# An attention kernel on one core: four key slots of one unit in four turned by DMA moves and VectorE instead of TensorE transposes

## What is computed

```python
# layer 0: x is (8, 512, 32, 32), 8 heads of 64 channels, n = 1024 pixels
hn = group_norm(x, gn1_scale, gn1_bias)
qkv = einsum('bchw,oc->bohw', hn, w_qkv) + b_qkv
q, k, v = split(qkv.reshape(b * 8, 3 * 64, n), 3, axis=1)
wgt = softmax(einsum('bct,bcs->bts', q * scale, k * scale), axis=-1)
a = einsum('bts,bcs->bct', wgt, v).reshape(b, c, h, w)
out = group_norm(einsum('bchw,oc->bohw', a, w_proj) + b_proj, gn2_scale, gn2_bias)
x = x + out
# layer 1: one head over 512 channels, weights normalised, RMS norm, residual
```

## Time and profile before

| | us |
|---|---|
| median of 3 runs | 3390.89 |
| lowest and highest | 3390.49, 3391.6 |
| the profiled execution | 3391.86 |
| its span, first to last instruction | 3389.7 |
| TensorE matmuls busy | 3361.0 |
| VectorE busy | 2125.2 |
| ScalarE busy | 1830.0 |
| GpSimd busy | 1063.3 |

### The profile page before, as it was taken

How to read it: one execution, slowest core, us unless ns; L and a number is a source line. 1 busy time by engine, 2 the same in 40 slices (tenths; PEclk the granted TensorE clock), 3 DMA queues, 4 the chain that set the end, 5 groups by cost and what they waited for, 6 DMA issues and landing times.

```text
span 3389.7 us, 51772 instructions
## 1 busy us (share of the span) xinstructions
PE 3361.0 (99%) x16752; PEld 2767.7 (82%) x16752; DVE 2125.2 (63%) x3468; ACT 1830.0 (54%) x3082; POOL 1063.3 (31%) x946
## 2 busy tenths in 40 slices
PE   7999999999999999999999999999999999999999
PEld 4888888888888888888888888888888888888887
DVE  4677456773578735786457864578555784557844
ACT  3677226772278623785237843388333883247822
POOL 0345113441044410354104531145211552124511
PEclk9999999999999999999999999999999999999999
DMA  8512245222544025341153322542224422343212
GB/s 322 164 38 63 94 124 138 67 59 78 134 120 95 32 93 150 88 100 74 45 157 99 82 75 64 155 100 63 78 76 141 100 63 94 86 140 74 63 56 75
DMA packets 109849, 332.10 MB, mean 98 GB/s; under 512 B 21744, under 2 KB 54768, under 8 KB 98800
## 3 DMA queue, kind: packets, MB, share of 16 engines
q1 hardware_dynamic: 107632, 322.15, 33.2%
q10 hardware_dynamic: 1920, 6.29, 0.9%
HBM read 162.68 MB, written 31.49 MB: 57 GB/s over the span
## 4 chain that ended last, share of the span: by engine, by line
PE 92%; DMA 2%; DVE 2%; ACT 1%; SPq 1%; issue 1%; POOL 0%; ACTq 0%; DVEq 0%; POOLq 0%
PE big L473 26%; PE big L606 14%; PE ops L592 14%; PE tps L577 14%; PE big L702 7%; PE big L613 5%; PE tps L773 4%; PE ops L773 4%; PE ops L556 3%; DMA ST<-ST 2%; PE big L516 1%; SPq L446 1%; DVE HL L1336 0%; DVE XA L1331 0%; SPq L389 0%
## 5 line engine op out<-in xcount | busy, mean ns | idle before, releaser
L1033 POOL TENSOR_SCALAR PB<-PB,small 128x1024 f32<-128x1024 f32 x576 | 648.1, 1125 | 1297.2 <-DVE small L1263 1279.4
L1257 DVE TENSOR_REDUCE small<-big 128x1 f32<-128x1024 f32 x512 | 625.0, 1221 | 85.1 <-PE big L606 82.0
L1268 DVE TENSOR_TENSOR PT<-tps,PT 128x512 fp32r<-128x512 f32 x1024 | 651.9, 678 | 42.0 <-ACT PT L894 41.7
L894 ACT ACTIVATE PT<-tps 128x512 fp32r<-128x512 f32 x1024 | 563.7, 596 | 159.2 <-PE tps L577 156.2
L888 ACT ACTIVATE PB<-big,small 128x1024 f32<-128x1024 f32 x512 | 572.2, 1118 | 93.6 <-DVE small L1257 90.6
L592 PE MATMUL ops<-PT,VT 128*128 128x512 f32 x2048 | 599.0, 414 | 0.0
L606 PE MATMUL big<-ST 128*128 128x512 f32 x2048 | 554.2, 392 | 2.7 <-DMA ST<-ST 2.7
L577 PEld LDWEIGHTS tps<-ident,PB 128*128 128x128 f32 x4096 | 470.3, 140 | 95.2 <-DVE PT L1268 31.3
L577 PE MATMUL tps<-ident,PB 128*128 128x128 f32 x4096 | 545.7, 274 | 0.9
L606 PEld LDWEIGHTS big<-ST 128*128 128x128 f32 x2048 | 382.6, 188 | 90.7 <-issue 5.5
L592 PEld LDWEIGHTS ops<-PT,VT 128*128 128x128 f32 x2048 | 346.1, 189 | 47.2 <-DVE PT L1268 5.0
(11 more groups left out here) (158 smaller groups left out, 4775.5 us busy)
## 6 DMA issues: line engine op xcount, KB each, us to landing
ST<-ST SPq DMA_DIRECT2D x360, 256.0 KB, 5.0
W<-d_qk SPq DMA_DIRECT2D x32, 1024.0 KB, 5.9
W<-PB SPq DMA_DIRECT2D x256, 128.0 KB, 2.4
XA<-in_x SPq DMA_DIRECT2D x8, 2048.0 KB, 7.6
X<-in_x SPq DMA_DIRECT2D x8, 2048.0 KB, 9.2
W<-d_wp SPq DMA_DIRECT2D x8, 2048.0 KB, 11.8
W<-d_g SPq DMA_DIRECT2D x8, 2048.0 KB, 12.2
W<-d_m SPq DMA_DIRECT2D x8, 2048.0 KB, 7.8
```

The source lines that it names most:

```text
L894: act_fn(pt_slot(u, s)[:, 0, :], tps[n % 2][:], ACT.Copy).then_inc(s_pt_hi, 1)
L1033: nc.gpsimd.tensor_scalar(PB[:, i, :], PB[:, i, :], rinv[:, i:i + 1], 1.0, ALU.mult, ALU.mult)\
L1257: V.tensor_reduce(negmax[:, i:i + 1], tile(("s", 4 * u + tb))[:], axis=AX.X, op=ALU.max, negate=True).then_inc(s_row_max, 1)
L1268: V.tensor_tensor(pt_slot(u, s)[:, 1, :], tps[n % 2][:], pt_slot(u, s)[:, 0, :].bitcast(f32), ALU.subtract).then_inc(s_pt_ready, 1)
```

## The change

Units 0, 4 and 8 of a batch (`MOVED`, the first unit of pairs 0 to 2) have their slots 4 to 7, the upper 512 keys, turned in another way. `move_quarters` lets SyncE issue, for each such unit, two parts of 16 transfers: part 0 when two blocks of probabilities are normalised, part 1 when all four are. One transfer copies 32 partitions by 2 blocks by 128 elements. They go from PB to F0, which is the lower half of X. When both parts are there, VectorE transposes in blocks of 32 (`square`) into the upper half of X: slots 4 and 5 in step 6 of the group of 16, slots 6 and 7 in step 8. `moved_hi` on ScalarE and `moved_lo` on VectorE then write the two parts in the same steps. TensorE skips the 16 transposes of these slots.

So that a row of 128 elements of a transfer holds what one partition quarter needs of all four slots, the upper 512 keys of pairs 0 to 2 are stored in another order (`keys_by_turn`): the four slots alternate with stride four. The other units of these pairs, which are still turned by TensorE, read their slots 4 to 7 with stride four.

X is now in use during pairs 0 to 2, so x is loaded behind slot 71 of the batch and behind `stack_head(b, 3, 0)`, and GpSimd scales it in steps 50, 52, 54 and 56.

```diff
+MOVED = [4 * pair for pair in range(PAIRS - 1)]
+MOVED_SLOTS = [8 * u + s for u in MOVED for s in range(4, NT)]
+def moved_pair(step):
+    n = 16 * (step // 16) + {6: 4, 8: 6}.get(step % 16, 0)
+    unit = 4 * (step // 16)
+    return (8 * unit + n % 16, 8 * unit + n % 16 + 1) if n % 16 and unit in MOVED else ()
-X_SCALE_STEPS = (20, 23, 26, 29)
+X_SCALE_STEPS = (50, 52, 54, 56)
+        F0 = X[:, 0:2, :].rearrange("p a (b n) -> p (a b) n", n=HALF).rearrange("p q (t n) -> p q t n", t=KB)
+        def squared(s):
+            return X[:, 2 + (s - 4) // 2, HALF * (s % 2):HALF * (s % 2) + HALF]
+        def keys_by_turn(pair, half, row):
+            if half and 4 * pair in MOVED:
+                return row.rearrange("p (q r s) -> p s q r", q=QUARTERS, s=4)
+            return row.rearrange("p (s q r) -> p s q r", q=QUARTERS, s=4)
+            def move_quarters(b, u):
+                for part in range(2):
+                    sp.wait_ge(s_p_norm, b * 72 + 4 * u + 2 * part + 2)
+                    own_wait(sp)
+                    if u and part == 0:
+                        sp.wait_ge(s_squared, squared_count(b, 8 * (u - 4) + NT - 1))
+                        own_wait(sp)
+                    rows = slice(2 * part, 2 * part + 2)
+                    for tq in range(QUARTERS):
+                        for sq in range(QUARTERS):
+                            sp.dma_start(F0[32 * sq:32 * sq + 32, tq, rows, :],
+                                         PB[32 * tq:32 * tq + 32, rows, HALF + P * sq:HALF + P * sq + P])\
+                              .then_inc(s_moved[part], 16)
-                sp.dma_start(X[:], src_x(b)).then_inc(s_x_res, 16)
+                move_quarters(b, 0)
                 sp.wait_ge(s_v_full, b * 4 + 4)
...
                 stack_head(b, 1, 1)
+                move_quarters(b, 4)
                 stack_head(b, 2, 0)
                 stack_head(b, 2, 1)
+                move_quarters(b, 8)
                 stack_head(b, 3, 0)
+                sp.wait_ge(s_pt_ready, b * 144 + MOVED_SLOTS[-1] + 1)
+                own_wait(sp)
+                sp.dma_start(X[:], src_x(b)).then_inc(s_x_res, 16)
...
-                                                   PB[:, 4 * (u % 2) + t, P * s:P * s + P], ident[:])
+                        row = PB[:, 4 * (u % 2) + t, :]
+                        if s >= 4 and u // 4 * 4 in MOVED:
+                            keys = row[:, HALF:N].rearrange("p (k s) -> p s k", s=4)[:, s - 4, :]
+                        else:
+                            keys = row[:, P * s:P * s + P]
+                        last = nc.tensor.transpose(tps[n % 2][:, P * t:P * t + P], keys, ident[:])
...
-                    if n >= 0:
+                    if n >= 0 and n not in MOVED_SLOTS:
                         transposes(n // 8, n % 8)
                         transposes(n // 8, n % 8 + 1)
...
                     if last_values(step):
                         last_v_hi(last_values(step))
+                    for n in moved_pair(step):
+                        moved_hi(n)
...
+                def square(n):
+                    u, s = n // 8, n % 8
+                    if s == 4:
+                        for part in range(2):
+                            dve.wait_ge(s_moved[part], (b * len(MOVED) + MOVED.index(u) + 1) * EXCHANGE)
+                    V.transpose(squared(s).rearrange("p (t q r) -> p t q r", t=KB, q=QUARTERS),
+                                F0.rearrange("p q t (r s) -> p s t q r", s=4)[:, s - 4, :, :, :])\
+                     .then_inc(s_squared, 1)
...
-                    if n >= 0:
+                    if n >= 0 and n not in MOVED_SLOTS:
                         pt_lo(n // 8, n % 8)
                         pt_lo(n // 8, n % 8 + 1)
+                    for n in moved_pair(step):
+                        square(n)
+                    for n in moved_pair(step):
+                        moved_lo(n)
```

More of the change, by code:

```diff
@@ L218, in build @@
         s_ld_u = sem("ld_u")
+        s_moved = [sem(f"moved{i}") for i in range(2)]
+        s_squared = sem("squared")
+        s_values_read = sem("values_read")
         s_stack_a = sem("stack_a")
@@ L574, in transposes @@
                     if n >= 2:
-                        pe.wait_ge(s_pt_ready, b * 144 + n - 1)
+                        bank_read = n - 2 if n - 2 not in MOVED_SLOTS else n - 6
+                        pe.wait_ge(s_pt_ready, b * 144 + bank_read + 1)
                     for t in range(4):
-                        last = nc.tensor.transpose(tps[n % 2][:, P * t:P * t + P],
-                                                   PB[:, 4 * (u % 2) + t, P * s:P * s + P], ident[:])
+                        row = PB[:, 4 * (u % 2) + t, :]
[4 more added lines that the diff above has]
+                        last = nc.tensor.transpose(tps[n % 2][:, P * t:P * t + P], keys, ident[:])
                     last.then_inc(s_t_full, 1)
@@ L593, in values0 @@
                                   start=(s == 0 and part == 0), stop=(s == 7 and part == 1))
+                    if n + 4 in MOVED_SLOTS:
+                        last.then_inc(s_values_read, 1)
                     if s == 7:
@@ L879, in qk_hi @@
                         act.wait_ge(s_stack_b, (b * PAIRS + pair) * 96)
-                    act_fn(unstacked(what, 0)[:, HALF * half:HALF * half + HALF], t[:, 0:HALF], ACT.Identity,
+                    to, of = unstacked(what, 0)[:, HALF * half:HALF * half + HALF], t[:, 0:HALF]
+                    if what:
+                        to, of = keys_by_turn(pair, half, to), of.rearrange("p (s q r) -> p s q r", q=QUARTERS, s=4)
+                    act_fn(to, of, ACT.Identity,
                            bias=(bq, bk)[what][:, pair:pair + 1])\
@@ L887, in exps @@
                     i = 4 * (u % 2) + tb
+                    if u - 2 in MOVED and tb == 0:
+                        for part in range(2):
+                            act.wait_ge(s_moved[part], (b * len(MOVED) + MOVED.index(u - 2) + 1) * EXCHANGE)
                     act_fn(PB[:, i, :], t[:], ACT.Exp, bias=negmax[:, i:i + 1], accum_out=rowsum[:, i:i + 1])\
@@ L1248, in qk_lo @@
                     cols = slice(HALF * half, HALF * half + HALF)
-                    V.scalar_tensor_tensor(unstacked(what, 1)[:, cols], tile(("qk", j))[:, 0:HALF],
-                                           (bq, bk)[what][:, pair:pair + 1],
-                                           unstacked(what, 0)[:, cols].bitcast(f32), ALU.add, ALU.subtract)\
-                     .then_inc(s_nat_ready, 1)
+                    to, of, hi = unstacked(what, 1)[:, cols], tile(("qk", j))[:, 0:HALF], unstacked(what, 0)[:, cols]
+                    if what:
+                        to, hi = keys_by_turn(pair, half, to), keys_by_turn(pair, half, hi)
+                        of = of.rearrange("p (s q r) -> p s q r", q=QUARTERS, s=4)
+                    V.scalar_tensor_tensor(to, of, (bq, bk)[what][:, pair:pair + 1], hi.bitcast(f32),
+                                           ALU.add, ALU.subtract).then_inc(s_nat_ready, 1)
                 def row_max(u, tb):
@@ L1269, in pt_lo, with moved_lo @@
                                     ALU.subtract).then_inc(s_pt_ready, 1)
+                def square(n):
+                    u, s = n // 8, n % 8
+                    if s == 4:
+                        for part in range(2):
+                            dve.wait_ge(s_moved[part], (b * len(MOVED) + MOVED.index(u) + 1) * EXCHANGE)
+                    V.transpose(squared(s).rearrange("p (t q r) -> p t q r", t=KB, q=QUARTERS),
+                                F0.rearrange("p q t (r s) -> p s t q r", s=4)[:, s - 4, :, :, :])\
+                     .then_inc(s_squared, 1)
+                def moved_lo(n):
+                    dve.wait_ge(s_pt_hi, b * 144 + n + 1)
+                    slot = pt_slot(n // 8, n % 8)
+                    V.tensor_tensor(slot[:, 1, :], squared(n % 8), slot[:, 0, :].bitcast(f32), ALU.subtract)\
+                     .then_inc(s_pt_ready, 1)
                 for j in range(4):
```

10 lines of the change are left out of this document (9 added, 1 removed).

## The result

The changed kernel takes 3683.59 us (median of 4 runs, 3682.62 to 3684.68) against 3391.09 us before; the ratio is 1.0862, with a 95% interval of 1.0845 to 1.0879. The forecast was 3628 us with a range of 3490 to 3735: slower, by the mechanism that was named, and 56 us short of the measured time. The range 3590 to 3665, which the prediction kept for the stall alone, was missed by 19 us; the measured time is nearer to 3692, halfway to its first rival, in which accesses with a stride pay as well.

A forecast was written before the change was run, and what follows sets the result against it. TensorE, busy 99% of the span, was taken as the bound. 3391.86 us plus 237 us of stall, with the 41.8 us gain inside, gave 3629, stated as 3628 because the profiled execution is 1.0 us above the median; range 3490 to 3735.

The forecast's parts named there:

- the stall alone: Main case: TensorE stalls for late moves at a pitch of 0.67 us, 3628 us, range 3590 to 3665, chance 0.45.
- first rival: The stall, and TensorE's strided transposes pay too: up to 3755 us, halfway 3692, chance 0.23.
- The bound and the mechanism: TensorE, busy 99% of the span, bounds the kernel; VectorE's squares wait for all 32 transfers, so TensorE stands still.
- The price of an issue: SyncE's 32 transfers per moved unit, priced from the second layer's exchange: pitch 0.672 us, landing 2.4 us after an issue starts.
- Rivals 2 and 3: Cheaper issues: pitch 0.53 us, 3506 to 3523 us (0.20 with nearby pitches); or moves hidden, 3350 us (0.07).
- The stall: TensorE idle 9.2 us before step 24's scores; units late by 11.0, 9.3 and 9.3 us per batch, 237 us in all.
- The strided writes: Upper keys written with stride four in step 11 of each pair: priced at nothing, at most 18 us.
- The strided reads: Stride-four reads by TensorE's transposes and VectorE's squares: priced at nothing, with 126 us and 34 us as upper ends.
- the prediction's own sign: Mean transpose above 272 ns in units 1 to 3 of a pair, or eight above 0.87 us, would mean rival 1 holds.
- rival 1: The stall, and strided transposes on TensorE pay, by up to 126 us: up to 3755 us, chance 0.23.
- rival 3: The moves are hidden and TensorE gains the full 41.8 us of skipped transposes: 3350 us, chance 0.07.
- Covered, as said: Weight loads of pairs 2 and 3, pair 2's stack transfers and the later x: hidden; late normalisations maybe a microsecond per batch.

The follow-up runs named there:

- e3: The change with one part of 16 transfers of 64 KB per moved unit, not two parts of 16 of 32 KB: 3523.23 us, ratio 1.0382.
- e4: The change with one transfer per part in place of 16, moved data mostly stale and output not right: 3427.02 us, ratio 1.01.
- e9: The change with keys stored as before; only score matmuls of moved units read upper keys in runs of 32, no stride four: 3637.21 us, ratio 1.0725.
- e1: The kernel before with only the new key order (strided key writes and transposes), no moves or squares: 3425.28 us, ratio 1.0096.
- e5: The change with keys in the old order; the last four value projections take every fourth pixel, so no strided writes: 3659.8 us, ratio 1.0782.
- e8: e4 with squares that read runs of 32 contiguous elements instead of every fourth one, data stale: 3408.79 us, ratio 1.0049.
- e10: e9's key order with moves through HBM, 12 issues per unit, and only units 4 and 8 moved: 3394.15 us, ratio 1.0007.
- e2: The kernel before with the 32 moves per unit issued and x loaded later, moved data unread, old key order: 3428.57 us, ratio 1.0112.
- e6: e5 with each part moved through HBM by 2 stores and 4 loads, 12 issues per unit instead of 32: 3448.12 us, ratio 1.0167.

## Why the prediction was right, and where it was short

**The bound and the mechanism: right.** TensorE's 99% were real, and what decides the change is the time at which the last of 32 transfers lands. e3 and e4 show it: 160 us less with half the issues, 257 us less with 2 of 32 (the stall of 234 to 248 us in the list of waits, and the half rate behind it).

**The price of an issue: right.** The pitch of 0.672 us was taken from the exchange; the new one is 0.597 us for the issue and about 0.64 in all. The 31 pitches and the landing made 23.2 us in the forecast; in unit 4 of batch 1 it was 629.39 to 651.3, 21.9 us. That is the shortest of the 24 units, whose mean is 22.9: in 18 of the 24 one issue lasts more than 1 us, up to 1.8, and this unit has none such. Unit 8 has one, in the chain of the change:

```profile
706.45 0.60 SPq L438
707.09 1.78 SPq L438
```

It takes 23.5 us from the first issue to the last landing, which is most of why its two steps are 11.2 us late instead of 9.0. Rivals 2 and 3 (a pitch of 0.53 or 0.40 us for smaller transfers) are refuted: a quarter of the bytes saves nothing of the issue.

**The stall: right in size.** TensorE stands 8.71 us in unit 4 (9.2 forecast), and the half rate afterwards makes 4 score matmuls last 2.08 us. The close agreement in unit 4 is partly luck: the data landed 1.3 us sooner than forecast, and the way from there to the scores took 4.2 us instead of 3.4. Sum of the three units 29.6 us forecast, 32.9 measured in the change, 30.2 in e9 without strides.

One row was misread, without harm. The low parts at 587.94 us, which the earlier trace rows and the prediction give to step 22, belong to step 21. Those of step 22 are

```profile
590.33 1.27 DVE L1268 TENSOR_TENSOR PT<-tps,PT 128x512 fp32r<-128x512 f32 x2
```

VectorE is free at 591.6 us, so the same forecast gives it a wait of 9.5 us and not 11.9. The 24 waits are 9.8 us on average (234.2 us). The sum does not use this term.

**The strided writes: the step that failed.** I wrote that they lie "in a step with room: nothing, at most 24 x 0.75 = 18 us". An operation takes 1.2 us instead of 0.69 or 0.75, and there are two in a row, high part before low part. That is 0.9 us late behind steps 12 and 28, by way of VectorE's low parts, and I had overlooked the start of a batch: there the keys of pair 0 are the last thing before the first stack transfer, with no cover at all. By the distances of e1 the writes cost 22 us, and e5, which has none, confirms the places.

**The strided reads: sized at nothing, with 126 us kept for TensorE and 34 for the squares.** TensorE's are 0.09 us per eight transposes, 144 groups of eight, so at most 13 us. By the prediction's own sign, more than 0.87 us for eight, rival 1 came true, at a tenth of its size. The squares took 1.08 us instead of 0.69, on the path behind the landing: the change less e9 is 46 us, of which e1's key order explains 32, so 14 are the squares' (a difference of two results, with no run of its own at the stall). With the writes these terms are 46 of the 56 us by which the forecast was short; e9, without them, is 9 us above it, about 5 of which are its three units (30.2 for 29.6 us in each batch). The Trainium skill, SBUF, the paragraph on cachelines, says that accesses which go to a new 16-byte line each time pay; the runs agree, strongly for ScalarE's write and VectorE's square (1.20 against 0.69, 1.08 against 0.69) and weakly for TensorE (0.96 against 0.87).

**What hides behind the stall, wrongly taken for granted.** The 41.8 us of rival 3 needed the other engines to follow a shorter step. They don't: without the stall the kernel is at e1's time (e4), so the least that this change could reach was not 3350 but about 3427. A sum of VectorE's work over the four steps was not made, and would not have settled it: from the earlier trace rows its row maxima, low parts and squares come to 14.6 us, overlaps not taken off, against 14.9 for TensorE, and e8, where VectorE is busy for 13.23 us, still lacks 25 of the 41.8 us. The waits in e4, e8 and e10 name single results that come late; how the loss divides among them, no run shows. And the wait of the exponential of unit u + 2 for the moves, which the diff adds, stood in no line of the prediction; by e2 it costs 36 us by itself, and beside the larger wait none is seen.

**Covered, as said:** the loads of weights, the later stack transfers and x. TensorE waits for stack transfers for 8.7 us instead of 2.7, but that is the start of a batch, by the strided writes: e1 has 9.3 us without any move, e9 2.8 us with all of them. The steps from 44 on have the old length, but for 0.1 us in those with strided transposes.

## What to carry to other kernels

A rearrangement by many small SBUF to SBUF transfers costs issues, not bytes: multiply the issue time by their number and hold it against the time from the first datum to the first reader, and look at everything queued behind the waiting instruction. Before work is shifted from a full engine to a helper, sum the helper's work over the few steps in which it must be done, and then ask for each result that stands behind the new work who reads it first. Here VectorE was busy for 14.55 of 15.96 us in e4, and the whole gain was lost without any long wait to show for it; with VectorE at 13.23 of 15.40 us (e8) more than half of it still was. If an operand needs another order, put it where an engine reads runs anyway (the moving operand of a few matmuls), not into a stored layout with a stride that all later writers and readers pay for.

## What the runs showed of the hardware

- An SBUF to SBUF transfer of 32 partitions has an issue of 0.597 us with 32 KB (the change), 0.601 us with 64 KB (e3) and 0.605 us with 128 KB, at a pitch of 0.64 to 0.67 us. In the change 18 of 768 issues last more than 1 us, up to 1.8.
- Through HBM, with two stores, a wait and four loads for each half, the same data land 13.3 to 15.7 us after the first issue (e6), against 21.9 to 23.6 us with 32 transfers inside SBUF: 12 issues for 32 took 212 us off the kernel (e6 against e5).
- Stride four in fp32 (16 bytes), for 128 x 512: a write by ScalarE 1.17 to 1.20 us against 0.69; VectorE's subtraction with such a write and one such read 1.13 to 1.20 against 0.75; VectorE's block transpose with such reads 1.08 against 0.69. TensorE's transposes: 0.96 us against 0.87 for eight. Score matmuls whose moving operand comes in runs of 32: in e9 a step of unit 0 is 0.02 to 0.05 us longer than before, one of unit 4 at most 0.01.
- After a stop of 8.7 us the granted clock was 0.50 and then 0.53, the 1.2 GHz level: 4 score matmuls took 2.08 us for 1.07 and the 4 value matmuls behind them 1.91 for 1.09 (e4); from 660 us on it was 1.00. At the start of the kernel the durations show the half rate (1057 for 592 ns) and the column doesn't.
